# A residual moved from a 128x128 fp32 matmul to two additions on VectorE, in a mixture-of-experts stage

## The chip, the cores and the metric

One core of one Trainium2 chip runs the whole kernel. The metric is device time in microseconds (us). Three runs of the kernel before took 1256.58, 1257.35 and 1257.95 us; their median is 1257.35.

## The reference, cut to what matters

A Mamba block (8 sequences of 1024 rows of 128 numbers) and then a transformer block are applied, each on a normed input, with an outer residual. The Mamba block is not touched by the change except in one preparing step. The transformer block is:

```python
y = layer_norm(x + mha(x), g1, be1)
z = layer_norm(y + moe(y), g2, be2)
# moe: idx = argmax(y @ Wg.T);  for the chosen e:  relu(y @ W1[e] + b1[e]) @ W2[e] + b2[e]
# outer: x = x + norm(z)            (norm without scale and shift)
```

So each row goes to one of 8 experts: 128 -> 512 -> 128, with two biases. What is summed per row is y + relu(y W1 + b1) W2 + b2. Here y = n * g1 + be1, where n is the row normed without scale and shift.

## The kernel before, in words

The five engines each run their own list of instructions: TensorE (PE), VectorE (DVE), ScalarE (ACT), GpSimd (POOL) and SyncE (SP), which issues most DMAs. They meet by semaphores: `wait_ge` holds an engine's whole list until a count is reached. The kernel has three parts: Mamba (to about 880 us), attention (groups of 4x128 rows, 16 groups) and experts.

Attention writes each row, normed but without scale and shift (n), with the row before it (x1) and its number, to a place in HBM (`routed`) that is ordered by expert (GpSimd's scatter, L1868). The experts then read tiles of 128 rows. There are 72 tiles, in 18 quads of 4. The order of the work is written out as slots: in slot s each engine issues its attention work of slot s and then its experts' work of slot s - 65 (`OVERLAP`), so the first experts' tiles run beside the last attention groups. Within an engine the order of the calls in `slot` is the order of issue. Slots of the experts are counted here from their own zero.

Scale and shift of the first norm are folded into the weights before: `fold_w1` into W1 and b1 (with a row of ones made by adding 1.0 to y's transposed copy, so that shifts divided by 128 and summed over 128 rows come out right), and the residual with scale, shift and b2 into one 128x128 fp32 matrix per expert, `w["residual"]` (`residual_base`, L1690 ff., and `residual_weights`, L1401 and L1703 ff.).

A tile t in the experts:

- `load_w1` (SP): copies W1 of the tile's expert to a ring of 4; `load_rows` loads a quad's rows (y, x1, number).
- `turn_y` (PE, L2027): transposes the tile to PSUM; it waits for the copy of the tile before. `copy_yT` (ACT, L2083) copies it to SBUF.
- `hidden` (PE, L2039): 4 fp32 matmuls; `relu` (ACT, L2090).
- `outward` (PE): first the residual matmul yT x `w["residual"]` of the expert (L2059), then 4 fp32 matmuls with W2 (L2063) on top of it, into a quarter of a PSUM bank (3 banks in turn).

Per quad q, from PSUM: `stats_a` (DVE, slot 6 + 4q; L2143 to L2154: four statistics, four aggregations, variance, mean), the inverse root (`root` on GpSimd, slot 8, L2224, for quads 0 to 14; for the last three ScalarE's root and Newton steps on VectorE, `invert`, L2182 ff.), `norm_a` (ACT, L2103, in halves in slots 9 and 10, PSUM -> `zn`), `affine` (DVE, slot 11, L2168 `zg` and L2172 `z`), `stats_b` (DVE, slot 12), root b (GpSimd, slot 13), `norm_b` (ACT, slots 15 and 16, L2114, `z_out`), `add_x1` (DVE, slot 17: `tokens` L2199 and `res` L2200, z_out + x1) and `scatter` (GpSimd, slot 17: 4 indirect DMAs, L2232, one per 128 rows; the indices are `tokens`).

In steady state VectorE's order per four slots is therefore: `stats_a`, `affine` (of the quad before), `stats_b` (of one more before), `add_x1` (of one more). GpSimd's is: root a, root b, four scatters.

Of the kernel before, what the change touches and what calls it, by code (L numbers as in the profile page):

```python
# [19 lines left out]
ALU = mybir.AluOpType  # L20
# [36 lines left out]
def mamba(nc, sem, carrier, banks, sel, ident, half_neg, x, w_in_t, conv_rows, per_channel, w_x_t, w_dt_t, w_out_t, x1, c_rows, late_loads, s_late,  # L57
# [8 lines left out]
    with ctx:  # L66
# [727 lines left out]
        def _(dve):  # L794
# [120 lines left out]
            def split_biases():  # L915

                bres = ygT[0:EXPERTS, :, :].rearrange("p t d -> p (t d)")[:, 0:DF + D]
                bmid = x1t[0:EXPERTS, :, :].rearrange("p t d -> p (t d)")[:, 0:(DF + D) // 2].bitcast(BF16)
                dve.memset(bias_parts[:, :], 0.0)
                dve.tensor_scalar(biases[:, :], biases[:, :], 1.0 / D, None, ALU.mult).then_inc(bias_chain, 1)  # L920
                dve.wait_ge(bias_chain, 1)
                dve.tensor_copy(bias_parts[0:EXPERTS, :], biases[:, :]).then_inc(bias_chain, 1)
                dve.wait_ge(bias_chain, 2)
                dve.tensor_tensor(bres, biases[:, :], bias_parts[0:EXPERTS, :], ALU.subtract).then_inc(bias_chain, 1)
                dve.wait_ge(bias_chain, 3)
                dve.tensor_copy(bmid, bres).then_inc(bias_chain, 1)
                dve.tensor_copy(bias_parts[32:32 + EXPERTS, :], bres).then_inc(bias_chain, 1)
                dve.wait_ge(bias_chain, 5)
                dve.tensor_tensor(bias_parts[64:64 + EXPERTS, :], bres, bmid, ALU.subtract).then_inc(bias_chain, 1)

# [170 lines left out]
def attention(nc, sem, carrier, banks, sel, ident, half_neg, w, shared, x1, v_rows, routed, expert_loads, sb, arena, front, S):  # L1101
# [39 lines left out]
    gap_cols = sb("shift_less_scale_cols", [P, P])  # L1141
    base = sb("residual_base", [P, D])
    gap_row = sb("shift_less_scale_row", [P, D])
    pk = sb("pk", [P, DEEP, GT, ROW])
# [124 lines left out]
    def tensor(pe):  # L1269
# [69 lines left out]
        def turn_y(j):  # L1339
            pe.wait_ge(S["r1_normed"], j + 1)  # L1340
            if j >= 1:
                pe.wait_ge(S["yT_copied"], j)
            else:
                pe.wait_ge(S["w1_folded"], EXPERTS + 2)
            if j == EARLY_GROUPS + 1:
                pe.wait_ge(S["early_chain"], 2)
            if j == EARLY_GROUPS + 2:
                pe.wait_ge(S["early_chain"], EARLY_STEPS)
            for i in range(GT):
                mm = pe.transpose(a3[:, i * P:(i + 1) * P], pk[:, j % DEEP, i, 0:D], ident[:, :])  # L1350
            mm.then_inc(S["y_transposed"], 1)

        def logits(j):
            pe.wait_ge(S["yT_copied"], j + 1)
            if j >= 1:
                pe.wait_ge(S["row_ids"], 5 * (j - 1) + 1)
            else:
                pe.wait_ge(S["gap_chain"], 7)
# [19 lines left out]
        def fold_gate():  # L1378
            pe.wait_ge(S["gap_chain"], 3)
            pe.wait_ge(S["w1_folded"], EXPERTS + 2)  # L1380
            pe.matmul(a2[:, 0:EXPERTS], gap_cols[:, :], w["wg"][:, :], start=True, stop=True)\
              .then_inc(S["weights_summed"], 1)

        def fold_w1(e):
# [5 lines left out]
            if e >= 2:  # L1390
# [4 lines left out]
              .then_inc(S["weights_summed"], 1)  # L1395

        def residual_weights(half):
            pe.wait_ge(S["w1_folded"], EXPERTS - 1 + half)
            for i in range(4):
                mm = pe.matmul((a2, a3)[half][:, i * D:(i + 1) * D], sel[:, 4 * half + i, :],  # L1400
                               w["bias_parts"][:, DF:], start=True, stop=True)  # L1401
            mm.then_inc(S["weights_summed"], 1)

# [31 lines left out]
        def slot(s):  # L1435
            if 0 <= s - 1 < EXPERTS:
                fold_w1(s - 1)
            if s in (9, 10):
                residual_weights(s - 9)
            if s == 16:  # L1440
# [125 lines left out]
    def vector(dve):  # L1566
# [117 lines left out]
        def fold_gate():  # L1684
            scale = w["norm1"][:, 0:1]
            dve.wait_ge(S["weights_summed"], EXPERTS + 3)
# [3 lines left out]
        def residual_base():  # L1690
            scale, shift = w["rows"][:, 2, :], w["rows"][:, 3, :]
            dve.tensor_tensor(gap_row[:, :], shift, scale, ALU.subtract).then_inc(S["gap_chain"], 1)
            dve.tensor_tensor(base[:, :], ident[:, :], scale, ALU.mult).then_inc(S["gap_chain"], 1)
            dve.wait_ge(S["gap_chain"], 5)
            dve.scalar_tensor_tensor(out=base[:, :], in0=gap_row[:, :], scalar=1.0 / D, in1=base[:, :], op0=ALU.mult,
                                     op1=ALU.add).then_inc(S["gap_chain"], 1)
# [6 lines left out]
        def residual_weights(half):  # L1703
            dve.wait_ge(S["gap_chain"], 6)
            dve.wait_ge(S["weights_summed"], EXPERTS + half + 1)
            dve.tensor_tensor(w["residual"][:, 4 * half:4 * half + 4, :],
                              (a2, a3)[half][:, :].rearrange("p (w d) -> p w d", w=4),
                              base[:, :].unsqueeze(1).broadcast_to([P, 4, D]), ALU.add).then_inc(S["w1_folded"], 1)

# [82 lines left out]
        def slot(s):  # L1792
# [94 lines left out]
def experts(nc, sem, banks, sel, ident, half_neg, w, shared, carrier, routed, out, sb, arena, R):  # L1887
# [65 lines left out]
    def sync(sp):  # L1953
# [27 lines left out]
        def load_w1(t):  # L1981
            q, i = divmod(t, 4)
            if t == 0:
                sp.wait_ge(R["w1_folded"], EXPERTS + 2)
                sp.sem_inc(carrier, 1)
# [28 lines left out]
    def tensor(pe):  # L2014
# [29 lines left out]
        def outward(t):  # L2044
            q, i = divmod(t, 4)
            if t == 0:
                pe.wait_ge(R["early_chain"], EARLY_STEPS)
                pe.wait_ge(R["experts_loaded"], 16)
                pe.wait_ge(R["w1_folded"], EXPERTS + 2)
# [28 lines left out]
    def scalar(act):  # L2078
# [18 lines left out]
        def norm_a(q, half):  # L2097
# [42 lines left out]
    def vector(dve):  # L2140
        def stats(src, stat, mv, var_eps, less_mean, s_bn, s_var, s_root, q):
# [3 lines left out]
            dve.wait_ge(s_bn, 2 * q + 1)  # L2145
            dve.sem_inc(carrier, 1)
# [103 lines left out]
def build(nc, x, w_in_t, conv_rows, per_channel, w_x_t, w_dt_t, w_out_t, wqkv_t, bqk, wo_t, wg_t, rows, biases, norm1, w1, w2,  # L2250
# [5 lines left out]
    with ExitStack() as ctx:  # L2256
# [17 lines left out]
        for name, n in TABLE:  # L2274
# [127 lines left out]
```

## Time and profile before

| | |
|---|---|
| three runs | 1256.58, 1257.35, 1257.95 us |
| span of the profiled execution | 1257.2 us (the page gives no other time of it) |
| busy: PE, DVE, ACT, POOL | 89%, 83%, 82%, 80% |
| experts | from about 1058 us (first `hidden`) to the end |
| L2059, residual matmul | x144 entries (two for each fp32 matmul), 27.8 us busy |
| L2232, scatters of the result | x72, 79.9 us busy, mean 1109 ns; 3% of the chain that ended last, its largest share |
| last 4 matmuls of the experts | start at 1225.19 us |
| last scatter | starts 1249.08 us |

The profile is one execution. Times in its rows are counted from the span's start. "Idle before" names what ended an engine's wait. An fp32 matmul has two entries. Entries of the same kind that follow one another are merged in a timeline, as "x4". The chain of waits is followed back from the last instruction, each time to what released it.

### The profile page before, as it was taken

To read this page: it belongs to the slowest core of one execution; us is meant where nothing else is said; L and a number is where in the kernel's file an instruction comes from. 1 tells how busy PE (TensorE), PEld (TensorE's weight loads), DVE (VectorE), ACT (ScalarE), POOL (GpSimd) and SP (SyncE) were. 2 spreads that over 40 slices of the span, in tenths; PEclk is the share of its full clock that TensorE was granted. 3 is DMA by queue.
4 is the path that set the end of the run, shared out by engine and by line. 5 is a ranking of instruction groups with operands and counts; after the bars stand their busy time and mean duration, and the time that the engine had idled before them with its cause. 6 is when DMAs were issued, how large, how long until landed. Compare 5 with 4: busy or idle time off the path is not lost. (4 is left out here: it accounts for less than half of the span.)

```text
span 1257.2 us, 29298 instructions
## 1 busy us (share of the span) xinstructions
PE 1122.1 (89%) x8868; PEld 939.1 (75%) x8868; DVE 1044.1 (83%) x2086; ACT 1025.8 (82%) x2140; POOL 1007.9 (80%) x825
## 2 busy tenths in 40 slices
PE   6799999999999999999999999877799997999990
PEld 2487877877878778787787877877466667989990
DVE  5599999999999999999999999996678887555564
ACT  4899899998998989989899899984479985556672
POOL 6498998989989889898898998986436776678875
PEclk9899999999999999999999999998799999999995
DMA  2223333333333232333333233341465556876640
GB/s 76 85 85 102 101 89 100 99 98 105 88 100 99 96 100 86 113 88 98 103 86 111 79 100 92 101 143 59 126 161 137 159 149 186 258 242 211 204 153 28
DMA packets 149637, 147.65 MB, mean 117 GB/s; under 512 B 46768, under 2 KB 99698, under 8 KB 149518
## 3 DMA queue, kind: packets, MB, share of 16 engines
q1 hardware_dynamic: 144142, 133.64, 36.5%
q0 software_dynamic: 5376, 12.63, 2.9%
q8 instruction: 50, 0.82, 0.3%
q14 instruction: 69, 0.57, 0.2%
HBM read 103.57 MB, written 23.24 MB: 101 GB/s over the span
## 5 line engine op out<-in xcount | busy, mean ns | idle before, releaser
L999 POOL TENSOR_TENSOR cm<-rows_or_blocks 128x1024 f32<-128x1024 f32 x256 | 618.1, 2423 | 81.4 <-DVE rows_or_blocks L834 76.2
L834 DVE TENSOR_TENSOR_SCAN rows_or_blocks<-abuf,hstate,bank 128x512 f32<-128x512 f32 x512 | 613.0, 1259 | 20.8 <-ACT abuf L668 7.4
L462 PE MATMUL bank<-ident,cm 128*128 128x128 f32 x2048 | 256.0, 273 | 2.8 <-POOL cm L999 2.7
L462 PEld LDWEIGHTS bank<-ident,cm 128*128 128x128 f32 x2048 | 230.3, 142 | 3.5 <-POOL cm L999 3.5
L668 ACT ACTIVATE abuf<-delta,aneg 128x512 f32<-128x512 f32 x256 | 166.8, 714 | 2.1 <-DVE rows_or_blocks L834 2.0
L668 ACT ACTIVATE abuf<-xg_or_delta,aneg 128x512 f32<-128x512 f32 x256 | 166.7, 714 | 0.0
L442 PE MATMUL bank<-ident,ub 128*128 128x128 f32 x1024 | 140.6, 279 | 27.1 <-ACT ub L679 16.7
L442 PEld LDWEIGHTS bank<-ident,ub 128*128 128x128 f32 x1024 | 115.7, 142 | 55.4 <-issue 25.7
L359 PE MATMUL bank<-xnT,rows_or_blocks 128*128 128x512 f32 x256 | 125.5, 607 | 1.0 <-ACT halo L596 1.0
L679 ACT ACTIVATE ub<-vs_or_uT,bT 128x256 f32<-128x256 f32 x256 | 108.7, 499 | 0.2
L679 ACT ACTIVATE ub<-uT,bT 128x256 f32<-128x256 f32 x256 | 108.6, 499 | 0.1
L2232 POOL DMA_INDIRECT out<-res,tokens x72 | 79.9, 1109 | 29.6 <-issue 26.6
L1848 POOL TENSOR_TENSOR b_rstd<-b_vare,half_neg 128x4 f32<-128x4 f32 x30 | 30.8, 1027 | 63.9 <-ACT xn_or_u L1483 47.3
L1868 POOL DMA_INDIRECT routed<-pk,desti x64 | 63.1, 986 | 20.3 <-issue 20.3
L2039 PE MATMUL bank<-d_yT,w_of_tile 128*128 128x128 f32 x576 | 76.4, 276 | 0.4 <-issue 0.3
L2063 PE MATMUL bank<-w,hT 128*128 x576 | 76.1, 275 | 0.0
L439 PEld LDWEIGHTS bank<-bdiag,vs_or_uT 128*128 128x128 f32 x512 | 62.1, 191 | 17.6 <-issue 9.1
L439 PEld LDWEIGHTS bank<-bdiag,uT 128*128 128x128 f32 x512 | 62.0, 192 | 16.4 <-issue 8.2
L439 PE MATMUL bank<-bdiag,vs_or_uT 128*128 128x128 f32 x512 | 65.4, 278 | 6.4 <-DVE rows_or_blocks L834 6.3
L2039 PEld LDWEIGHTS bank<-d_yT,w_of_tile 128*128 128x128 f32 x576 | 70.3, 192 | 0.8 <-issue 0.8
L2063 PEld LDWEIGHTS bank<-w,hT 128*128 128x128 f32 x576 | 70.1, 192 | 0.0
L439 PE MATMUL bank<-bdiag,uT 128*128 128x128 f32 x512 | 64.8, 278 | 5.9 <-DVE rows_or_blocks L834 5.9
(298 smaller groups left out, 2114.6 us busy)
## 6 DMA issues: line engine op xcount, KB each, us to landing
rows_or_blocks<-c_rows SPq DMA_DIRECT2D x256, 256.0 KB, 3.2
w_of_tile<-w SPq DMA_DIRECT2D x72, 256.0 KB
rows_or_blocks<-routed SPq DMA_DIRECT2D x72, 128.5 KB
xin<-in_x SPq DMA_DIRECT2D x16, 256.0 KB, 3.6
xres<-in_x SPq DMA_DIRECT2D x16, 256.0 KB, 3.8
x_rows<-x1t SPq DMA_DIRECT2D x16, 256.0 KB, 3.5
xg_or_delta<-x_rows SPq DMA_DIRECT2D x16, 256.0 KB, 3.7
v_rows<-vs_or_uT SPq DMA_DIRECT2D x16, 256.0 KB, 3.4
```

The costliest lines, as they stand in the source:

```text
L359: mm = pe.matmul(bank_xc(f, c)[:, :], w_tap[:, k, c * P:(c + 1) * P], xnT[:, parity(f), k:k + HALF], start=k == 0, stop=k == TAPS - 1)
L439: mm = pe.matmul(dst, uT[parity(g)][:, j, c * P:(c + 1) * P], bdiag[:, n // 4 % 2, j, :], start=True, stop=True)
L442: mm = pe.transpose(dst, ub[:, n // 2 % 2, j, c * P:(c + 1) * P], ident[:, :])
L462: mm = pe.matmul(ps_y[j // 2][:, (j % 2 * CH + c) * P:(j % 2 * CH + c + 1) * P], cm[:, n % CM_RING, c, j * P:(j + 1) * P], ident[:, :], is ...
L668: e = act.activation(abuf[:, n % RING, c, :], delta[parity(g)][:, c, :], ACT.Exp, scale=aneg[:, c, n:n + 1])
L679: i = act.activation(ub[:, n // 2 % 2, j, :], uT[parity(g)][:, j, :], ACT.Copy, scale=bT[:, parity(g), j, n:n + 1])
L834: dve.tensor_tensor_scan(hbuf[:, n % RING, c, :], abuf[:, n % RING, c, :], ps_bx[n % 2 * CH + c][:, :], hstate[:, bass.ds(g * (NST * CH) + ...
L999: pool.tensor_tensor(cm[:, n % CM_RING, :, :], hbuf[:, n % RING, :, :], c, ALU.mult).then_inc(s_cm, 1)
L1868: pool.indirect_dma_start(out=routed[:, :], out_offset=bass.IndirectOffsetOnAxis(ap=desti[:, j % DEEP, i:i + 1], axis=0), in_=pk[:, j % DE ...
L2039: mm = pe.matmul(ps_h[t % 2][:, k * P:(k + 1) * P], w1[:, t % W1_RING, k * P:(k + 1) * P], yT[:, t % YT_RING, :], start=True, stop=True)
L2063: mm = pe.matmul(dst, hT[:, t % 2, k, :], w["w2"][:, bass.ds(e[t], 1), k, :].rearrange("p o d -> p (o d)"), start=False, stop=k == DF // P ...
L2232: pool.indirect_dma_start(out=out[:, :], out_offset=bass.IndirectOffsetOnAxis(ap=tokens[:, q % 2, i:i + 1], axis=0), in_=res[:, q % 2, i, ...
```

## The change

The residual is no longer multiplied. VectorE scales the quad's rows by g1 (`scale_rows`, slot 5 + 4q, after `stats_a` and ahead of `add_x1` in its order) and adds the result to the quad's sums from PSUM (`add_rows`, slot 6 + 4q, ahead of `stats_a`). The row of shifts, be1 + b2[e], is now split into three bf16 parts, stacked at partitions 0, 32 and 64, and added by one bf16 matmul per tile whose stationary operand, `sel`, picks the expert's rows (96 x 128 by 96 x 128). `stats_a` and `norm_a` read the sum from SBUF. The making of the fp32 residual weights in the attention part goes; `split_second_biases` comes (slot 11 of the attention): an addition, a copy, a subtraction, two copies and a subtraction, 8x128 each. `residual_base` was three 128x128 operations on VectorE, `residual_weights` twice 4 bf16 matmuls and a 128x512 addition.

```diff
+        def split_second_biases():
+            chain, parts, second = S["gap_chain"], w["bias_parts"][:, DF:], w["biases"][:, DF:]
+            dve.tensor_tensor(second, second, w["rows"][0:EXPERTS, 3, :], ALU.add).then_inc(chain, 1)
...
-            if s == 6:
-                residual_base()
+            if s == 11:
+                split_second_biases()
-            if s in (10, 11):
-                residual_weights(s - 10)
@@ outward
-                    pe.wait_ge(S["zn_ready"], q - 2)
+                    pe.wait_ge(S["stats_a"], 4 * (q - 2))
             dst = ps_f[q % 3][:, i * D:(i + 1) * D]
-            pe.matmul(dst, yT[:, t % YT_RING, :], w["residual"][:, bass.ds(e[t], 1), :].rearrange("p o d -> p (o d)"),
+            pe.matmul(dst, sel[:, bass.ds(e[t], 1), :].rearrange("p o t -> p (o t)"), w["bias_parts"][:, DF:],
                       start=True, stop=False)
@@ norm_a
-                a = act.activation(zn[:, q % 2, i, :], ps_f[q % 3][:, i * D:(i + 1) * D], ACT.Identity,
+                a = act.activation(zn[:, q % 2, i, :], summed[:, q % 2, i, :], ACT.Identity,
@@ vector
+        def scale_rows(q):
+            n = 4
+            if q == 0:
+                for i in range(4):
+                    dve.wait_ge(S[f"w1_loaded{i}"], 32)
+            else:
+                dve.wait_ge(s_rows[q % 4], 64 * (q // 4 + (q % 4 > 0)))
+                dve.wait_ge(S["stats_a"], 4 * q)
+            dve.tensor_tensor(scaled[:, 0:n, :], rows[:, q % RINGS, 0:n, 0:D],
+                              w["rows"][:, 2, :].unsqueeze(1).broadcast_to([P, n, D]), ALU.mult)\
+               .then_inc(S["stats_a"], 1)
+
+        def add_rows(q):
+            n = 4
+            dve.wait_ge(S["expert_summed"], 4 * q + n)
+            dve.wait_ge(S["stats_a"], 4 * q + 1)
+            if q >= 2:
+                dve.wait_ge(S["zn_ready"], q - 1)
+            dve.tensor_tensor(summed[:, q % 2, 0:n, :], ps_f[q % 3][:, 0:n * D].rearrange("p (i d) -> p i d", i=n),
+                              scaled[:, 0:n, :], ALU.add).then_inc(S["stats_a"], 1)
+
         def stats_a(q):
-            dve.wait_ge(S["expert_summed"], 4 * (q + 1))
+            dve.wait_ge(S["stats_a"], 4 * q + 2)
@@ slot of the experts on VectorE
             for q in due(s, 6):
+                add_rows(q)
                 stats_a(q)
+            for q in due(s, 5):
+                scale_rows(q)
             for q in due(s, 17):
                 add_x1(q)
```

At the start of the kernel the split of the biases (`split_biases`, L914 ff.) now covers the first biases alone, 8x512 instead of 8x640; waits for `w1_folded` ask for 8 instead of 10.

## Rows read from the trace of the kernel before

**Rows 1.** Table by stretch: stretch, length, busy of each engine, clock, DMA share, GB/s

```profile
1066.00:1113.00 47.00, 46.21 (x420) 45.35 (x420) 27.81 (x164) 26.83 (x67) 31.23 (x35) 1.00 0.78 248
...
1157.00:1210.00 53.00, 52.44 (x460) 51.31 (x459) 30.90 (x144) 35.64 (x96) 42.77 (x49) 1.00 0.62 207
```

**Rows 2.** Timeline of GpSimd: start, duration, engine, line, operation, [idle before]

```profile
1113.03 1.05 POOL L2224 TENSOR_TENSOR d_rstd_a<-d_vare_a,half_neg 128x4 f32<-128x4 f32 x1
...
1161.53 1.31 POOL L2232 DMA_INDIRECT out<-res,tokens  x1 [0.30 <-issue]
...
1164.42 1.37 POOL L2232 DMA_INDIRECT out<-res,tokens  x1 [0.30 <-issue]
...
1209.79 1.05 POOL L2224 TENSOR_TENSOR d_rstd_a<-d_vare_a,half_neg 128x4 f32<-128x4 f32 x1
```

**Rows 3.** Timeline of VectorE, the period at 1157

```profile
1160.57 0.69 DVE L2168 TENSOR_TENSOR zg<-zn,row_params 128x512 f32<-128x512 f32 x1 [1.57 <-ACT zn L2103]
1161.29 0.69 DVE L2172 TENSOR_TENSOR z<-zg,row_params 128x512 f32<-128x512 f32 x1
...
1163.61 0.16 DVE L2154 TENSOR_SCALAR d_nmean_b<-d_mv_b 128x4 f32<-128x4 f32 x1
1164.18 0.17 DVE L2199 COPY tokens<-rows_or_blocks 128x4 int32<-128x4 int32 x1 [0.41 <-ACT z_out L2114]
1164.26 0.69 DVE L2200 TENSOR_TENSOR res<-z_out,rows_or_blocks 128x512 f32<-128x512 f32 x1
```

**Rows 4.** Timeline of ScalarE, same period

```profile
1158.37 0.81 ACT L2103 ACTIVATE zn<-bank,d_shift_a,d_rstd_a 128x128 f32<-128x128 f32 x2 [1.67 <-POOL d_shift_a L2226]
1159.07 0.28 ACT L2083 ACTIVATE d_yT<-bank 128x128 f32<-128x128 f32 x1
...
1161.16 0.87 ACT L2114 ACTIVATE z_out<-z,d_shift_b,d_rstd_b 128x128 f32<-128x128 f32 x2
1161.93 0.26 ACT L2083 ACTIVATE d_yT<-bank 128x128 f32<-128x128 f32 x1
```

**Rows 5.** Timeline of TensorE: the table's matmul at 1101, and one tile

```profile
1101.64 0.17 PE L1423 MATMUL bank<-cum_h,ones 128*128 128x8 bf16 x1
...
1101.82 1.06 PE L2039 MATMUL bank<-d_yT,w_of_tile 128*128 128x128 f32 x8
...
1161.58 0.27 PE L2027 MATMUL bank<-ident,rows_or_blocks 128*128 128x128 f32 x1
...
1162.59 0.39 PE L2059 MATMUL bank<-residual_weights,d_yT 128*128 x2
1162.81 1.06 PE L2063 MATMUL bank<-w,hT 128*128 x8
1163.70 0.27 PE L2027 MATMUL bank<-ident,rows_or_blocks 128*128 128x128 f32 x1
```

**Rows 6.** Timeline of GpSimd, where its last wait of the early stage ends

```profile
1100.11 1.52 POOL L2224 TENSOR_TENSOR d_rstd_b<-d_vare_b,half_neg 128x4 f32<-128x4 f32 x1 [2.70 <-ACT z_out L2114]
```

**Rows 7.** Timeline of all engines at 922, attention

```profile
922.57 0.42 PEld L1275 LDWEIGHTS bank<-ident,xn_or_u 128*128 128x128 f32 x4 [0.20 <-ACT xn_or_u L1483]
```

**Rows 8.** Timeline of all engines at 979, attention

```profile
979.45 0.69 DVE L1613 TENSOR_TENSOR o<-bank,rs 128x512 f32<-128x512 f32 x1
979.51 0.96 POOL L1868 DMA_INDIRECT routed<-pk,desti  x1 [0.30 <-issue]
```

**Rows 9.** Timeline of all engines at 1235, the last quads

```profile
1234.97 0.73 DVE L2168 TENSOR_TENSOR zg<-zn,row_params 128x512 f32<-128x512 f32 x1
1234.98 0.97 POOL L2232 DMA_INDIRECT out<-res,tokens  x1 [2.03 <-DVE res L2200]
```

**Rows 10.** Timeline of VectorE, the last quads

```profile
1223.53 0.18 DVE L2182 RECIPROCAL d_guess_a<-d_spread_a 128x4 f32<-128x4 f32 x1 [0.80 <-ACT d_spread_a L2095]
...
1233.42 0.69 DVE L2200 TENSOR_TENSOR res<-z_out,rows_or_blocks 128x512 f32<-128x512 f32 x1
1234.02 0.17 DVE L2182 RECIPROCAL d_guess_b<-d_spread_b 128x4 f32<-128x4 f32 x1
```

More of the change, by code:

```diff
@@ L915, in split_biases @@
             def split_biases():
-                bres = ygT[0:EXPERTS, :, :].rearrange("p t d -> p (t d)")[:, 0:DF + D]
-                bmid = x1t[0:EXPERTS, :, :].rearrange("p t d -> p (t d)")[:, 0:(DF + D) // 2].bitcast(BF16)
+                bres = ygT[0:EXPERTS, :, :].rearrange("p t d -> p (t d)")[:, 0:DF]
+                bmid = x1t[0:EXPERTS, :, :].rearrange("p t d -> p (t d)")[:, 0:DF // 2].bitcast(BF16)
+                first, parts = biases[:, 0:DF], bias_parts[:, 0:DF]
                 dve.memset(bias_parts[:, :], 0.0)
-                dve.tensor_scalar(biases[:, :], biases[:, :], 1.0 / D, None, ALU.mult).then_inc(bias_chain, 1)
+                dve.tensor_scalar(first, first, 1.0 / D, None, ALU.mult).then_inc(bias_chain, 1)
                 dve.wait_ge(bias_chain, 1)
-                dve.tensor_copy(bias_parts[0:EXPERTS, :], biases[:, :]).then_inc(bias_chain, 1)
+                dve.tensor_copy(parts[0:EXPERTS, :], first).then_inc(bias_chain, 1)
                 dve.wait_ge(bias_chain, 2)
-                dve.tensor_tensor(bres, biases[:, :], bias_parts[0:EXPERTS, :], ALU.subtract).then_inc(bias_chain, 1)
+                dve.tensor_tensor(bres, first, parts[0:EXPERTS, :], ALU.subtract).then_inc(bias_chain, 1)
                 dve.wait_ge(bias_chain, 3)
                 dve.tensor_copy(bmid, bres).then_inc(bias_chain, 1)
-                dve.tensor_copy(bias_parts[32:32 + EXPERTS, :], bres).then_inc(bias_chain, 1)
+                dve.tensor_copy(parts[32:32 + EXPERTS, :], bres).then_inc(bias_chain, 1)
                 dve.wait_ge(bias_chain, 5)
-                dve.tensor_tensor(bias_parts[64:64 + EXPERTS, :], bres, bmid, ALU.subtract).then_inc(bias_chain, 1)
+                dve.tensor_tensor(parts[64:64 + EXPERTS, :], bres, bmid, ALU.subtract).then_inc(bias_chain, 1)
             dve.memset(w_x[:, :, RANK:BROW], 0.0)
@@ L1141, in attention @@
     gap_cols = sb("shift_less_scale_cols", [P, P])
-    base = sb("residual_base", [P, D])
-    gap_row = sb("shift_less_scale_row", [P, D])
+    bres = sb("bias_rest", [EXPERTS, D])
+    bmid = sb("bias_middle", [EXPERTS, D], BF16)
     pk = sb("pk", [P, DEEP, GT, ROW])
@@ L1343, in turn_y @@
             else:
-                pe.wait_ge(S["w1_folded"], EXPERTS + 2)
+                pe.wait_ge(S["w1_folded"], EXPERTS)
             if j == EARLY_GROUPS + 1:
@@ L1357, in logits @@
             else:
-                pe.wait_ge(S["gap_chain"], 7)
+                pe.wait_ge(S["gap_chain"], 10)
             for i in range(GT):
@@ L1395, in fold_w1 @@
               .then_inc(S["weights_summed"], 1)
[L1397 to L1402, printed above, removed]
         def early_table(part):
@@ L1437, in slot @@
                 fold_w1(s - 1)
-            if s in (9, 10):
-                residual_weights(s - 9)
             if s == 16:
@@ L1685, in fold_gate @@
             scale = w["norm1"][:, 0:1]
-            dve.wait_ge(S["weights_summed"], EXPERTS + 3)
+            dve.wait_ge(S["weights_summed"], EXPERTS + 1)
             dve.scalar_tensor_tensor(out=gate[:, :], in0=w["wg"][:, :], scalar=scale, in1=a2[:, 0:EXPERTS],
                                      op0=ALU.mult, op1=ALU.add).then_inc(S["gap_chain"], 1)
[L1690 to L1696, printed above, removed]
+        def split_second_biases():
+            chain, parts, second = S["gap_chain"], w["bias_parts"][:, DF:], w["biases"][:, DF:]
+            dve.tensor_tensor(second, second, w["rows"][0:EXPERTS, 3, :], ALU.add).then_inc(chain, 1)
+            dve.wait_ge(chain, 4)
+            dve.tensor_copy(parts[0:EXPERTS, :], second).then_inc(chain, 1)
+            dve.wait_ge(chain, 5)
+            dve.tensor_tensor(bres[:, :], second, parts[0:EXPERTS, :], ALU.subtract).then_inc(chain, 1)
+            dve.wait_ge(chain, 6)
+            dve.tensor_copy(bmid[:, :], bres[:, :]).then_inc(chain, 1)
+            dve.tensor_copy(parts[32:32 + EXPERTS, :], bres[:, :]).then_inc(chain, 1)
+            dve.wait_ge(chain, 8)
+            dve.tensor_tensor(parts[64:64 + EXPERTS, :], bres[:, :], bmid[:, :], ALU.subtract).then_inc(chain, 1)
         def fold_w1(e):
@@ L1701, in fold_w1 @@
                                      in1=(a2, a3)[e % 2][:, :], op0=ALU.mult, op1=ALU.add).then_inc(S["w1_folded"], 1)
[L1703 to L1708, printed above, removed]
         def clear_small():
@@ L1901, in experts @@
     hT = sb("hT", [P, 2, DF // P, P])
+    scaled = sb("rows_scaled", [P, 4, D])
+    summed = sb("rows_and_expert", [P, 2, 4, D])
     zn = sb("zn", [P, 2, 4, D])
@@ L1983, in load_w1 @@
             if t == 0:
-                sp.wait_ge(R["w1_folded"], EXPERTS + 2)
+                sp.wait_ge(R["w1_folded"], EXPERTS)
                 sp.sem_inc(carrier, 1)
@@ L2048, in outward @@
                 pe.wait_ge(R["experts_loaded"], 16)
-                pe.wait_ge(R["w1_folded"], EXPERTS + 2)
+                pe.wait_ge(R["gap_chain"], 9)
             if t == EARLY_TILES:
@@ L2140, in vector, with stats @@
     def vector(dve):
-        def stats(src, stat, mv, var_eps, less_mean, s_bn, s_var, s_root, q):
+        def stats(src, stat, mv, var_eps, less_mean, s_bn, at, s_var, s_root, q):
             for i in range(4):
@@ L2144, in stats @@
             b.then_inc(s_bn, 1)
-            dve.wait_ge(s_bn, 2 * q + 1)
+            dve.wait_ge(s_bn, at + 1)
             dve.sem_inc(carrier, 1)
@@ L2151, in stats @@
                 dve.wait_ge(s_root, root_steps(q))
-            dve.wait_ge(s_bn, 2 * q + 2)
+            dve.wait_ge(s_bn, at + 2)
             dve.tensor_scalar(var_eps[:, :], mv[:, :, 1], EPS, None, ALU.add)
             dve.tensor_scalar(less_mean[:, :], mv[:, :, 0], -1.0, None, ALU.mult).then_inc(s_var, 1)
+        def scale_rows(q):
[17 more added lines that the diff above has]
+                              scaled[:, 0:n, :], ALU.add).then_inc(S["stats_a"], 1)
         def stats_a(q):
-            dve.wait_ge(S["expert_summed"], 4 * (q + 1))
-            stats(lambda i: ps_f[q % 3][:, i * D:(i + 1) * D], stat_a, mv_a, vare[0], nmean[0], S["stats_a"],
+            dve.wait_ge(S["stats_a"], 4 * q + 2)
+            stats(lambda i: summed[:, q % 2, i, :], stat_a, mv_a, vare[0], nmean[0], S["stats_a"], 4 * q + 2,
                   S["variance_a"], S["roots_a"], q)
@@ L2175, in stats_b @@
             dve.wait_ge(S["z_ready"], q + 1)
-            stats(lambda i: z[:, q % 2, i, :], stat_b, mv_b, vare[1], nmean[1], S["stats_b"], S["variance_b"],
+            stats(lambda i: z[:, q % 2, i, :], stat_b, mv_b, vare[1], nmean[1], S["stats_b"], 2 * q, S["variance_b"],
                   S["roots_b"], q)
```

3 lines of the change are left out of this document (1 added, 2 removed).

## The prediction

> **What bounds the kernel now.** I read the page first, then the table by stretch, the chain of waits, and then the timelines of single engines. The change touches the experts alone (1058 us to the end) and a few instructions of the attention. In the table TensorE looks like the bound of both long stretches of the experts: busy 46.21 of 47 us at first, 52.44 of 53 us later [rows 1]. That is true of the first only. From 1113 us on the chain of waits runs over GpSimd: its eleven rounds from root to root last (1209.79 - 1113.03) / 11 = 8.80 us per quad of four tiles [rows 2], while TensorE needs 4 x 2.12 = 8.48 us for them [rows 5]. TensorE is slowed to that pace through ScalarE, which stands still 1.67 us a round before `zn` for GpSimd's root [rows 4], with the next `copy_yT` queued behind it.
>
> GpSimd is not simply full. Two of its four scatters last 1.31 and 1.37 us [rows 2]; undisturbed ones last 0.97 us [rows 9]. The first of the two starts 0.24 us after `z` started on VectorE and the second 0.16 us after `res` [rows 3]: both start while VectorE adds two operands from SBUF, and both end 0.85 us after that addition does. So the round is a loop through both engines. From the start of the root: 1.37 to `zn` (1158.37 against 1157.00, one round before 1165.80, where the fourth scatter ends), 2.20 to `zg`, 0.72 to `z`, 2.32 to the last of `stats_b`, 0.57 to `tokens` (0.41 of it a wait for `z_out`), 0.08 to `res`, 0.69 for it, 0.85 to the scatter's end: 8.80 us [rows 2 to 4].
>
> **The change, part by part.** Terms are against the profiled span of 1257.2 us; the runs' median, 1257.35, lies 0.15 above it, and I add the sum to the median.
>
> *TensorE.* The residual's fp32 matmul takes 1162.81 - 1162.59 = 0.22 us of a tile of 2.12; four fp32 ones take 0.89, so the turn takes 0.12 [rows 5]. No bf16 matmul of 128 columns between fp32 ones is shown. The nearest is the table's of 8 columns: with it the turn and it take 0.18, so it costs 0.06, and the other 120 columns at 2.4 GHz (granted clock 1.00) are at most 0.05 more. I take 0.09, a gain of 0.13 a tile (bounds 0.10 and 0.16). It counts only where TensorE sets the pace, up to GpSimd's last real wait, 2.70 us for `z_out` of the first quad [rows 6]; from there GpSimd is loaded without a gap. That `z_out` stands in slot 16 of the experts, after 15 tiles' sums; the first two tiles' gain runs into the wait for the loaded rows of the second quad. 13 x 0.13 = 1.7 us; the DMA engines are 0.78 busy here [rows 1] and the faster tiles will meet some waits, so I take 1.3 us (0.5 to 2.1). From there to the end TensorE's gain is worth nothing: it ends in a longer wait.
>
> *ScalarE.* `norm_a` reads SBUF instead of PSUM. From `zn`'s first half to the next instruction it is 0.70 us, from `z_out`'s, which reads SBUF, 0.77 [rows 4]. With half of that again in the second half `zg` comes 0.11 later.
>
> *VectorE, per round.* `scale_rows` has two operands from SBUF like `z`, so 0.69 us, and the next instruction starts 0.60 after it [rows 10]. In VectorE's order it stands behind `stats_b` and ahead of `add_x1`: `tokens` and `res` are queued behind it, and the scatter waits for them. It waits for nothing itself. `add_rows` costs 0.72 (0.69 and the step to `stats_a`, as from `zg` to `z` [rows 3]). Before `stats_a` VectorE waits for TensorE, and the variance that it gives is used a round later, so `add_rows` is hidden; its cover is the 1.57 us of wait before `zg` [rows 3], and without it, it would cost 0.72 a round. `scale_rows` is not hidden: it takes the 0.41 us wait before `tokens` and more. The loop becomes 1.37 + 2.31 + 0.72 + 2.32 + 0.08 + 0.60 + 0.08 + 0.69 + 0.85 = 9.02 us, 0.22 more than now, 11 times: +2.4 us (bounds in the rivals: -0.3 and +0.6 a round).
>
> A two-operand addition holds up GpSimd. The one from PSUM doesn't: `o` started 0.06 before a scatter, ran 0.63 into it, and that lasted 0.96 [rows 8]. The Trainium skill ("SBUF — State Buffer", Who interferes with whom) draws the same line: VectorE with two SBUF inputs contends with a GpSimd instruction that reads SBUF, with one input it does not. It also infers that such an addition leaves the writing of DMA descriptors alone; by that half the scatters would not be delayed, a round would stay at 8.80 and the sum would be +0.6. The 1.37 beside 0.97 us speaks against it: an indirect DMA has indices to read.
>
> *The end.* From quad 15 on the roots leave GpSimd and VectorE is full, but for 0.80 us [rows 10], until `res` of quad 15; the last twelve scatters start 0.87 us after that (1234.98 against 1234.11) and run in a row [rows 9, 10]. Two `scale_rows` and two `add_rows` fall into this stretch, 2 x 0.60 + 2 x 0.72 = 2.6 us, `zn` adds 0.1, and the 0.80 takes part of it: +1.9 us (1.2 to 2.7). TensorE's earlier end is no help, since the sums wait for VectorE then.
>
> *Attention.* Gone are eight small bf16 matmuls, two additions of 0.69 us like `o` [rows 8], three 128x128 operations; six 8x128 ones come, at 0.16 to 0.2 each [rows 3]. They lie where the next turn on TensorE waits for ScalarE's `xn` anyway [rows 7], and `less_max` behind them has room. I take 0, between -0.8 (all removed work on the path) and +1.2 (all of the new). The start-up's narrower splits lie ahead of a wait of VectorE: 0.
>
> Sum: -1.3 + 2.4 + 1.9 = +3.0, so 1260.3 us.
>
> **Rivals.** *GpSimd reads first (not slower).* The place is the fourth scatter of the round. It starts 3.13 after `z` started (1164.42 - 1161.29) and will again, since it hangs on the second scatter, which ends with `z`; `res` starts now at 2.97 and then at 2.32 + 0.08 + 0.60 + 0.08 = 3.08: only 0.05 ahead instead of 0.16. At 0.16 VectorE wins [rows 2, 3]; at 0.01 GpSimd won, with 0.97 us [rows 9]. The point from which it decides lies between. If GpSimd wins, the round is 8.80 - 0.34 - 0.40 + 0.45 = 8.5 us (both lengthenings gone, the first back and 0.11 longer): 11 x -0.3 = -3.3, and -1.3 - 3.3 + 1.9 = -2.7: 1254.7. For it: the margin is as small as my error. Against: the margin is still on VectorE's side. The skill's page (same section) says that whichever starts first keeps the port for its whole instruction, which would have VectorE win here, 1260.3.
> *The addition from PSUM contends too.* It would lie over the next root: up to 0.4 a round, 11 x 0.4 = 4.4 more: 1264.7. Rows 8 speak against it.
> *The bf16 matmul gives nothing*, because the fp32 weights behind it load no faster: no 1.3 at the start, 1261.6. The 0.06 of the table's matmul speaks against it.
> *The new addition falls where no scatter starts*, and `res` keeps its place: a round stays at 8.80, +0.6, 1258.0. Against it is the order on VectorE.
>
> **How the numbers follow.** Forecast 0.48 (its own range 1258.3 to 1262.3), GpSimd first 0.27, PSUM contends 0.07, no gain of the matmul 0.08, round unchanged 0.10. The range of 8 in 10 reaches to the faster case and leaves out most of the PSUM case: 1253.8 to 1262.6. About 0.2%, 2.5 us, can be told from no change. Slower by more: 0.3 of the forecast's 0.48, and the two cases above it, 0.44. Faster by more: 0.2 of the second case's 0.27 and a little of the last, 0.22. The rest, 0.34, is the same.
>
> **What would show it.** TensorE's tile at 1.99 us in the early stretch; GpSimd's last early wait ending 1.3 us sooner; rounds of 9.0 us with a fourth scatter of some 1.5 us, with `tokens` right behind `scale_rows` and no wait; `zg` 2.31 behind `zn`; `zn` rows near 0.48; no wait of VectorE from quad 15's root to `res` 15, and that 1.9 us later against the last root on GpSimd. A fourth scatter of 0.97 would be the first rival; a root of 1.4 the second. Wrong altogether I would be if the rounds left GpSimd, with TensorE or VectorE full instead.

## The result, and the profile after

The changed kernel takes 1260.98 us (median of 12 runs, 1258.75 to 1262.97) against 1256.96 of the kernel before (12 runs, 1254.83 to 1258.81): ratio 1.003, interval 1.0021 to 1.0038, so 4.0 us slower, between 2.6 and 4.8. Forecast was 1260.3, 3.0 us slower. The profiled execution after took 1261.45 us with a span of 1259.6. In every later run whose span is on record the time is 1.7 to 1.9 us above the span, so the profiled execution of the kernel before, with its span of 1257.2, took about 1259.0 us (an estimate): 2.0 more than the median of its runs.

The table by stretch, after (columns as in [rows 1]):

```profile
1066.00:1113.00 47.00, 43.61 (x401) 42.94 (x401) 33.33 (x166) 26.73 (x67) 31.79 (x36) 1.00 0.78 249
1157.00:1210.00 53.00, 48.77 (x428) 47.35 (x427) 37.48 (x156) 36.05 (x96) 42.83 (x48) 1.00 0.61 204
```

TensorE has lost 2.6 and 3.7 us of work in the two stretches, VectorE has gained 5.5 and 6.6; GpSimd has the same 42.8 us in the second. Why TensorE's relief doesn't show in the time can be read from one round, that is from one root a to the next (root a is the inverse root of `stats_a` on GpSimd, once per quad). Timelines of one round, after: first GpSimd's (start, duration, engine, line, operation),

```profile
1156.61 1.05 POOL L2238 TENSOR_TENSOR d_rstd_a<-d_vare_a,half_neg 128x4 f32<-128x4 f32 x1
...
1161.13 1.43 POOL L2246 DMA_INDIRECT out<-res,tokens  x1 [0.30 <-issue]
1162.86 0.98 POOL L2246 DMA_INDIRECT out<-res,tokens  x1 [0.30 <-issue]
1164.14 1.48 POOL L2246 DMA_INDIRECT out<-res,tokens  x1 [0.30 <-issue]
1165.62 1.07 POOL L2238 TENSOR_TENSOR d_rstd_a<-d_vare_a,half_neg 128x4 f32<-128x4 f32 x1
```

then VectorE's,

```profile
1156.33 0.69 DVE L2164 TENSOR_TENSOR rows_and_expert<-bank,rows_scaled 128x512 f32<-128x512 f32 x1 [0.58 <-PE bank L2053]
...
1160.29 0.69 DVE L2179 TENSOR_TENSOR zg<-zn,row_params 128x512 f32<-128x512 f32 x1 [1.48 <-ACT zn L2093]
1161.02 0.69 DVE L2183 TENSOR_TENSOR z<-zg,row_params 128x512 f32<-128x512 f32 x1
...
1163.41 0.69 DVE L2154 TENSOR_TENSOR rows_scaled<-rows_or_blocks,row_params 128x512 f32<-128x512 f32 x1
1164.01 0.16 DVE L2210 COPY tokens<-rows_or_blocks 128x4 int32<-128x4 int32 x1
1164.08 0.68 DVE L2211 TENSOR_TENSOR res<-z_out,rows_or_blocks 128x512 f32<-128x512 f32 x1
```

then ScalarE's and TensorE's.

```profile
1157.97 0.88 ACT L2093 ACTIVATE zn<-rows_and_expert,d_shift_a,d_rstd_a 128x128 f32<-128x128 f32 x2 [2.05 <-POOL d_shift_a L2240]
1158.76 0.26 ACT L2073 ACTIVATE d_yT<-bank 128x128 f32<-128x128 f32 x1
```

```profile
1162.14 0.22 PE L2049 MATMUL bank<-bias_parts,sel 96*128 96x128 bf16 x1
1162.20 1.11 PE L2053 MATMUL bank<-w,hT 128*128 x8
1163.14 0.27 PE L2017 MATMUL bank<-ident,rows_or_blocks 128*128 128x128 f32 x1
...
1165.15 0.27 PE L2017 MATMUL bank<-ident,rows_or_blocks 128*128 128x128 f32 x1
```

A round is 1165.62 - 1156.61 = 9.01 us. `scale_rows` (L2154) has pushed `tokens` and `res` back, the wait before `tokens` in [rows 3] is gone, `res` starts 0.06 ahead of the fourth scatter, and this scatter lasts 1.48 us; the second scatter, 0.11 behind the start of `z`, lasts 1.43. Both end 0.86 and 0.85 us after the addition. `add_rows` (L2164) stands behind a wait of 0.58: hidden. ScalarE's wait for the root has grown from 1.67 to 2.05 us: TensorE's relief ends in a longer wait.

Not every round is like this one. Of the eleven, four at the start take 8.50, 9.15, 8.52 and 9.57 us, six take 9.01 to 9.03, and one takes 8.66: there `res` comes 0.26 behind the fourth scatter, and this lasts 1.12. I call the ones of 9.01 to 9.03 settled.

The landmarks of both kernels, each profiled twice (the second pair, `g1` and `g2`, ran on one chip; it is told below), in us; "root a 3" is the start of root a of quad 3, and the eleven rounds go from there to root a 14:

| | first tile's turn | root a 3 | root a 14 | last scatter | span |
|---|---|---|---|---|---|
| before, rows 1 to 10 | 1056.9 | 1113.03 | 1209.79 | 1249.08 | 1257.2 |
| after | 1056.2 | 1111.84 | 1210.36 | 1251.49 | 1259.6 |
| before again (`g1`) | 1055.6 | 1111.54 | 1205.05 | 1245.83 | 1254.0 |
| after again (`g2`) | 1054.8 | 1110.03 | 1208.24 | 1249.37 | 1257.5 |

First pair: -1.2 up to root a 3, +1.8 in the rounds, +1.8 in the end, sum +2.4. Second pair: -1.5, +4.7, +0.3, sum +3.5. The sums are the differences of the spans. The last scatters of after (GpSimd) and what they wait for (VectorE):

```profile
1237.41 0.97 POOL L2246 DMA_INDIRECT out<-res,tokens  x1 [2.75 <-DVE res L2211]
...
1251.49 0.97 POOL L2246 DMA_INDIRECT out<-res,tokens  x1 [0.30 <-issue]
```

```profile
1235.78 0.16 DVE L2210 COPY tokens<-rows_or_blocks 128x4 int32<-128x4 int32 x1
1235.85 0.69 DVE L2211 TENSOR_TENSOR res<-z_out,rows_or_blocks 128x512 f32<-128x512 f32 x1
```

`res` of quad 15 is 25.49 us behind root a 14; it was 23.63 in [rows 2, 10].

### The profile page after: what moved, and what is told of

It reads as the page before. It is cut to its first block and busy times, and to the rows that moved or that the text cites. A ratio compares the mean times of both kernels' runs of the same rounds, so it can differ in the third digit from the quotient of the medians.

```text
span 1259.6 us, 29210 instructions
## 1 busy us (share of the span) xinstructions
PE 1116.4 (89%) x8788; PEld 933.0 (74%) x8788; DVE 1065.3 (85%) x2123; ACT 1027.4 (82%) x2140; POOL 1011.3 (80%) x825
## 5 line engine op out<-in xcount | busy, mean ns | idle before, releaser
L1836 POOL TENSOR_TENSOR b_rstd<-b_vare,half_neg 128x4 f32<-128x4 f32 x30 | 30.7, 1023 | 65.3 <-ACT xn_or_u L1475 43.7
L2053 PE MATMUL bank<-w,hT 128*128 x576 | 80.7, 284 | 0.0
```

The lines of the kernel that those rows point to most:

```text
L2053: mm = pe.matmul(dst, hT[:, t % 2, k, :], w["w2"][:, bass.ds(e[t], 1), k, :].rearrange("p o d -> p (o d)"), start=False, stop=k == DF // P ...
```

## The experiments

**The theory:** an instruction of GpSimd that starts just after a VectorE addition of two SBUF operands is held up until some 0.85 us after that addition's end; the change costs 0.22 us a round because `scale_rows` lengthens the loop that goes through this. **The rival:** the round is longer because VectorE's chain is, wherever `res` falls.

Edits are shown against the changed kernel where nothing else is said.

**On two slower chips.** The first eight kernels ran on chips on which the kernel before takes 1299.86 us (the four of `e`; median of 35 runs) and 1306.5 us (the four of `f`; 35 runs). Single runs of one kernel differ by up to 18 us there, so an interval is 5 to 8 us wide and can't show the 1 to 3 us that most of the expectations speak of.

*The matmul alone* (`e1`, repeated as `f1`). The residual is left out of the computation, neither multiplied nor added:

```diff
-                    pe.wait_ge(S["stats_a"], 4 * (q - 2))
+                    pe.wait_ge(S["zn_ready"], q - 2)
...
-                a = act.activation(zn[:, q % 2, i, :], summed[:, q % 2, i, :], ACT.Identity,
+                a = act.activation(zn[:, q % 2, i, :], ps_f[q % 3][:, i * D:(i + 1) * D], ACT.Identity,
...
-                add_rows(q)
                 stats_a(q)
-            for q in due(s, 5):
-                scale_rows(q)
```

`stats_a` reads the sums from PSUM again, too.

> The changed kernel without scale_rows and add_rows: the bf16 one-hot matmul stays, stats_a and norm_a read PSUM again, so the output lacks the residual. Theory of three terms (start -1.3, rounds +0.22 x 11, end +1.9, the last two by VectorE's additions): only the start's gain is left. The round at GpSimd is 8.80 us again, the tile of TensorE about 2.0 us, the total 1 to 2 us under the kernel before (some 1255.6), with the last scatter 1 to 2 us earlier than before. Rival (TensorE sets the pace of the experts after all, as its busy share says): 72 tiles x 0.11 us = 8 us under the kernel before. Rival (the fall of TensorE's clock to 0.50 near 1115 us, after a longer idle time, costs time): it is here too, and the kernel is no faster than before.

> The kernel of e1_matmul_only once more, on another chip: there the kernel before took 1300 us, TensorE stood still for 0.7 us a quad at its table of experts, and rounds of 10 us hid what was to be seen. The expectation is the same: about 1.3 us under the kernel before if only the start's gain is left, rounds of 8.80 us, tile of 2.0 us; 8 us under it if TensorE set the pace.

Measured: 1298.7 us, 0.9986 (0.9954 to 1.0018), and 1305.2, 0.9996 (0.9968 to 1.0023): neither can be told from no change. 8 us less, as the rival of `e1` has it, is excluded.

*`scale_rows` a quad early* (`e2`, `f2`), right behind `stats_a` of the quad before, so that it no longer stands between `stats_b` and `tokens`:

```diff
+                if q == 0:
+                    scale_rows(0)
                 add_rows(q)
                 stats_a(q)
-            for q in due(s, 5):
-                scale_rows(q)
+                if q + 1 < QUADS:
+                    scale_rows(q + 1)
```

> The changed kernel with one move: scale_rows of the next quad is issued right behind stats_a, where VectorE waits for zn (1.48 us), instead of between stats_b and add_x1. Same work, same result. Theory (its place in the loop is what it costs): tokens waits for z_out again, the round goes from 9.02 back to about 8.85 us, 11 rounds give 1.5 to 2 us, and the end some 0.6: 2 to 2.5 us under the changed kernel. Rival (VectorE's load as such costs): same time as the changed kernel within 0.5 us.

> The kernel of e2_scale_early once more. Theory (place in the loop): rounds of about 8.85 instead of 9.02 us, 2 to 2.5 us under the changed kernel, so 0.1% over the kernel before. Rival (load as such): 0.3% over it, as the changed kernel.

Measured: 1299.48, 1.0005 (0.9979 to 1.003), and 1304.41, 0.9981 (0.9959 to 1.0003): neither can be told from no change.

*`res` later than the scatter's start* (`e3`, `f3`), by two idle statistics on VectorE behind `tokens`:

```diff
+            if q < BY_POWER:
+                for k in range(2):
+                    dve.bn_stats(spare[:, k, :], w["rows"][:, 4, :])
```

> The changed kernel with more work on VectorE: two statistics of a constant 128x128 tile (0.2 us each) between tokens and res, quads 0 to 14. Theory (GpSimd's fourth scatter is held up because res starts just before it): res now starts 0.35 us after that scatter, which takes 0.97 instead of 1.48 us; the round falls from 9.02 to about 8.5 us and the total by 4 to 5.5 us, to about 1256. Rival (no such hold-up; VectorE's chain is simply longer): 0.4 us more a round, 11 x 0.4 = 4.4 us slower than the changed kernel.

> The kernel of e3_res_late once more. Theory (hold-up of the fourth scatter): rounds of about 8.5 us, the fourth scatter 0.97 us, 1 us under the kernel before. On the slow chip both lengthenings were gone and it was the only one clearly under the kernel before (0.9961). Rival (longer chain): rounds of 9.4 us, 8 us over the kernel before.

Measured: 1295.29, 0.9961 (0.9936 to 0.9986), and 1299.94, 0.996 (0.9932 to 0.9987). With more work on VectorE this is the only version whose interval lies below the kernel before there, both times: the rival, which asked for 8 us over it in `f3`, is wrong there too. Why it is below isn't shown, since its rounds (9.9 to 10.0 us) are not the expected 8.5.

*The additions alone* (`e4`). The one-hot matmul is replaced by an fp32 one of the old size, so the sum is another one:

```diff
-            pe.matmul(dst, sel[:, bass.ds(e[t], 1), :].rearrange("p o t -> p (o t)"), w["bias_parts"][:, DF:],
+            pe.matmul(dst, yT[:, t % YT_RING, :], w["w2"][:, bass.ds(e[t], 1), 0, :].rearrange("p o d -> p (o d)"),
```

> The changed kernel with a 128x128 fp32 matmul in the place of the bf16 one (yT by the first quarter of W2 of the expert, so its sum is wrong): VectorE's additions alone, TensorE as before. Theory of three terms: the start's gain goes, rounds and end stay: about 1.3 us over the changed kernel, some 5.3 over the one before; tile of TensorE 2.12 us, round 9.0 us. Rival (TensorE's gain is worth more than the start): 3 us or more over the changed kernel.

Measured: 1302.38, 1.0014 (0.9983 to 1.0044): no change that can be told.

*The kernel before with `res` late* (`f5`), the same two statistics.

> The kernel before, its residual by the fp32 matmul, with only the same two idle statistics (0.2 us each) between tokens and res, quads 0 to 14. Theory: the fourth scatter takes 0.97 instead of 1.37 us, the round falls from 8.80 to TensorE's 8.48 us: 11 x 0.3 = 3.3 us under the kernel before, although VectorE only does more. Rival (no hold-up): 0 to 4.4 us over it.

Measured: 1307.23, 1.0014 (0.9993 to 1.0035): not the 3.3 us less that the theory gave.

On these chips the rounds are another matter: 9.9 to 10.6 us on the mean (root a 3 to root a 14) instead of the 8.5 to 9.02 of the expectations, bound by something that the first chip doesn't show. `e1`, TensorE from 1110 to 1250 us by groups (busy, mean ns, idle before and its releasers), and one of its rows:

```profile
L2053 PE MATMUL bank<-w,hT 128*128 x424 | 60.1, 285 | 4.4 <-issue 4.4
L2017 PE MATMUL bank<-ident,rows_or_blocks 128*128 128x128 f32 x53 | 15.6, 294 | 19.7 <-ACT d_yT L2073 19.7
```

```profile
1130.67 1.15 PE L2053 MATMUL bank<-w,hT 128*128 x8 [1.59 <-issue]
```

and `f5`, the same groups of the kernel before:

```profile
L2064 PE MATMUL bank<-w,hT 128*128 x408 | 57.0, 284 | 20.0 <-ACT hT L2091 12.6 <-issue 7.3
```

TensorE stands still ahead of `outward` with no releaser to be seen, 0.7 to 1.6 us at a time, in both kernels; after, on the first chip, has 0.0 there in the same stretch. What it waits for stays open, and it is the smaller part: these waits are 4.4 us in `e1`, those for `d_yT` 19.7 (9.0 in after, on the first chip). What these runs do tell: `e1` and `f1` need 41.95 and 41.96 us from root a 14 to the last scatter, `e2`, `f2` and `e4` with the additions 43.8 to 44.3, so the two passes on VectorE cost some 2 us in the end stage. (`f5`, with the fp32 matmul and idle statistics, needs 47.59; the kernel before itself has no profile there.) They don't price the rounds, neither for the theory nor against it, so I went back to a chip like the first.

**On a chip like the first** (kernel before: 1256.39 us, 29 runs), all four together. *Both kernels unchanged* (`g1` one execution, `g2`).

> The kernel before, for a second profile beside the next three. Theory, if this chip runs it in about 1257 us: rounds of 8.80 us, second and fourth scatter 1.3 and 1.37 us. If it runs it in 1300 us as the chips of the runs so far, TensorE stands still at the first residual matmul of a quad and the rounds are 10 us or more, set by TensorE; then the lengthened scatters are rare, and this profile is the base for the others.

> The changed kernel once more. On a chip like the first: +3 us, rounds of 9.02, start 1.2 earlier, end 1.9 later. On a slow chip, where TensorE sets the rounds: the rounds cost nothing (or gain the matmul's 0.1 us a tile, up to 5 us in all), the end still costs 1.9 us: ratio 0.997 to 1.002. Rival (the additions cost wherever they stand, by VectorE's load): 1.003 there too.

Measured: `g1` 1255.74; `g2` 1259.91, 1.0025 (1.0015 to 1.0036). The changed kernel has the rounds of its first profile: 8.93 on the mean, 9.00 to 9.03 when settled, and again a single one of 8.65. The kernel *before* does not: its eleven rounds take 8.50 instead of 8.80. The chain that ended last, its share by engine, from the page of the first profile of before and from that of `g1`:

```profile
PE 7%; issue 7%; POOL 6%; ACT 5%; DVE 2%; SPq 1%; DMA 1%; POOLq 0%; ACTq 0%; DVEq 0%
```

```profile
PE 15%; ACT 5%; issue 3%; DVE 3%; POOL 1%; DMA 1%; POOLq 0%; SPq 0%; DVEq 0%; ACTq 0%
```

One round of `g1`, GpSimd, VectorE and ScalarE:

```profile
1154.18 1.06 POOL L2224 TENSOR_TENSOR d_rstd_a<-d_vare_a,half_neg 128x4 f32<-128x4 f32 x1
...
1158.71 1.40 POOL L2232 DMA_INDIRECT out<-res,tokens  x1 [0.30 <-issue]
...
1161.69 0.97 POOL L2232 DMA_INDIRECT out<-res,tokens  x1 [0.30 <-issue]
1162.67 1.06 POOL L2224 TENSOR_TENSOR d_rstd_a<-d_vare_a,half_neg 128x4 f32<-128x4 f32 x1
```

```profile
1158.56 0.69 DVE L2168 TENSOR_TENSOR zg<-zn,row_params 128x512 f32<-128x512 f32 x1 [0.55 <-ACT zn L2103]
...
1162.87 0.19 DVE L2199 COPY tokens<-rows_or_blocks 128x4 int32<-128x4 int32 x1 [1.09 <-ACT z_out L2114]
1162.95 0.68 DVE L2200 TENSOR_TENSOR res<-z_out,rows_or_blocks 128x512 f32<-128x512 f32 x1
```

```profile
1157.73 0.80 ACT L2103 ACTIVATE zn<-bank,d_shift_a,d_rstd_a 128x128 f32<-128x128 f32 x2
...
1161.97 0.87 ACT L2114 ACTIVATE z_out<-z,d_shift_b,d_rstd_b 128x128 f32<-128x128 f32 x2
```

`res` starts 8.77 us after root a, where it was 1164.26 - 1157.01 = 7.25 in the round of [rows 3]. It comes only when the fourth scatter is done, and this lasts 0.97. GpSimd then needs 8.49 us (8.06 and one lengthening of 0.43), TensorE 4 x 2.12 = 8.48, and `zn` has no wait for the root: TensorE paces ScalarE, ScalarE's `z_out` keeps `res` back. So the kernel before has two patterns with the same code. The expectation of `g1`, rounds of 8.80 with a long fourth scatter, was wrong.

*`res` late in the changed kernel* (`g3`, the edit of `e3`).

> The kernel of e3_res_late a third time, for the first time beside the changed kernel. Theory (hold-up): fourth scatter 0.97 us; on a chip like the first rounds of 8.5 us and 4 to 5 us under the changed kernel, on a slow one 0 to 3 us under it. Rival (longer chain): over the changed kernel by 4 us on a chip like the first, by 0 to 4 on a slow one.

Measured: 1259.24, 1.0018 (1.0007 to 1.0028): 0.7 us under the changed kernel, where 4 to 5 were expected. The round is as expected. One of them, GpSimd and VectorE:

```profile
1166.84 1.42 POOL L2250 DMA_INDIRECT out<-res,tokens  x1 [0.30 <-issue]
1168.56 0.97 POOL L2250 DMA_INDIRECT out<-res,tokens  x1 [0.30 <-issue]
1169.83 0.97 POOL L2250 DMA_INDIRECT out<-res,tokens  x1 [0.30 <-issue]
1170.81 1.07 POOL L2242 TENSOR_TENSOR d_rstd_a<-d_vare_a,half_neg 128x4 f32<-128x4 f32 x1
```

```profile
1169.12 0.69 DVE L2155 TENSOR_TENSOR rows_scaled<-rows_or_blocks,row_params 128x512 f32<-128x512 f32 x1
...
1169.79 0.48 DVE L2214 BATCH_NORM_STATS2 spare<-row_params 128x6 f32<-128x128 f32 x2
1170.19 0.73 DVE L2215 TENSOR_TENSOR res<-z_out,rows_or_blocks 128x512 f32<-128x512 f32 x1
```

VectorE does 0.4 us more in a round, `res` starts 0.36 behind the fourth scatter, this lasts 0.97, and the round falls from 9.01 to 8.50 (1162.31 to 1170.81). The rival is refuted for the round: with its longer chain the round would have grown. Over eleven rounds it is 8.60 on the mean, 3.7 us less than `g2`; but the end stage takes 42.27 instead of 41.13 (the last of the idle statistics fall into it) and the start 0.5 more. The profiled span is 2.0 us shorter; the medians of `g3` and `g2` differ by 0.7 only (the means by 1.4), with runs of `g3` from 1256.95 to 1260.98, so the profiled run, 1257.29, is one of its faster ones. The cause is shown in the rows and hardly in the time.

*Both meetings avoided* (`g4`): `e2`'s move, two idle statistics between `zg` and `z`, two before `res`.

> The changed kernel with scale_rows of the next quad behind stats_a, two idle statistics between zg and z, and two between tokens and res, quads 0 to 14: neither z nor res then starts just before a scatter. Theory: all four scatters 0.97 to 1.04 us, rounds of about 8.1 us on a chip like the first (GpSimd's own time, 8.80 - 0.34 - 0.40), 10 us under the changed kernel and 6 under the one before; on a slow one the fastest of the four all the same. Rival: 0.8 us more of VectorE's work a round costs up to 9 us.

Measured: 1258.82, 1.0015 (1.0006 to 1.0024): 1.1 us under the changed kernel instead of 10. Rounds of 8.06 us appear, with all scatters after the first at 0.97: GpSimd's own time. But every second round or so is 9.1 to 9.5. Where it goes wrong, GpSimd and VectorE:

```profile
1166.89 0.97 POOL L2255 DMA_INDIRECT out<-res,tokens  x1 [0.31 <-issue]
1167.87 1.32 POOL L2247 TENSOR_TENSOR d_rstd_a<-d_vare_a,half_neg 128x4 f32<-128x4 f32 x1
...
1171.33 1.21 POOL L2255 DMA_INDIRECT out<-res,tokens  x1 [0.62 <-issue]
```

```profile
1167.62 0.67 DVE L2218 TENSOR_TENSOR res<-z_out,rows_or_blocks 128x512 f32<-128x512 f32 x1
...
1170.93 0.69 DVE L2155 TENSOR_TENSOR rows_scaled<-rows_or_blocks,row_params 128x512 f32<-128x512 f32 x1
```

`res` now meets the root (1.32 instead of 1.05, it started 0.25 after `res`) and the moved `scale_rows`, 0.40 ahead, the first scatter (1.21 instead of 1.04). Fixed padding doesn't hold the two engines apart; with a mean round of 8.65 and a start 3.5 us longer than in `g2` (1056.9 to 1115.63), nothing is won. No version tried beats the kernel before on this chip. `e2`'s move alone and `f5`'s late `res` in the kernel before were not run on this chip, so that `scale_rows` costs by its place in the loop rests on the rows of the round and on no run of its own.

## Why the prediction was right, point by point

- **Start, -1.3.** A tile on TensorE takes 2.01 us, not 1.99: the fp32 matmuls start 0.06 after the bf16 one, but take 0.94 instead of 0.89, so it costs 0.11 where I took 0.09. Up to root a 3 the profiles are 1.2 and 1.5 us earlier, but 0.7 and 0.8 of that is there before the experts' first tile. I put attention at 0, and two profiles of the kernel before differ by 1.3 at the same point, so that part can't be told from no change. Within the experts it is -0.5 and -0.7: over-sized. In the first pair the second quad waits longer for its rows, 2.14 us instead of 0.45; the second pair doesn't show that wait.
- **Rounds, +0.22.** Every term of the loop came out: `zn` 1.36 after the root's start, `zg` 2.32 after that, `tokens` 0.60 and `res` 0.67 behind `scale_rows`, the scatter's end 0.86 after `res`'s: 9.02 predicted, 9.00 to 9.03 in the settled rounds of two profiles. That five of eleven rounds are others makes the term +1.8 instead of +2.4 in the first pair. `g3` shows that the hold-up is the cause of the long fourth scatter. It was the comparison that failed: I took 8.80 as *the* round of before, from one profile in which it is constant. In `g1` it is 8.50, and the term is +4.7.
- **Which starts first.** I put `res` 0.05 ahead of the fourth scatter; it is 0.06, and VectorE wins. The margin was as thin as I feared: in the six profiles of the two faster chips a scatter that starts 0.01 or 0.02 behind such an operation lasts 0.96 or 0.97, all that start 0.04 to 0.49 behind are lengthened, and of three at 0.03 two are (1.50 and 1.51) and one is not (0.98). The first rival (round 8.5) is thus wrong for the changed kernel, but its pattern, a fourth scatter of 0.97, is the one in which the kernel *before* runs in `g1`, only with `res` behind that scatter, not beside it. The Trainium skill ("SBUF — State Buffer", Who interferes with whom) infers that such additions leave the writing of DMA descriptors alone; here the scatter's 1.48 us with `res` 0.06 ahead of it, against 0.97 with `res` 0.36 behind (`g3`), says otherwise for an indirect DMA with its indices in SBUF. The Trainium skill ("SBUF — State Buffer", Summary: rules for kernel authors) also says that with two SBUF inputs against a GpSimd instruction that reads SBUF the second to start is blocked until the first is done. Here that holds one way only: where GpSimd is first, VectorE's instruction isn't held, and takes 0.67 to 0.75 us beside a scatter (`res` 0.73 in the round of `g3`) against 0.67 to 0.69 alone.
- **`add_rows` and the PSUM rival.** It starts 0.28 ahead of root a, which lasts 1.05: no contention. `res`, two operands from SBUF, 0.25 ahead of the root in `g4` makes it 1.32. The second rival is wrong.
- **"The matmul gives nothing"** is wrong too: 0.11 a tile, and [rows 5]'s turn to turn of 2.12 is now 2.01.
- **End, +1.9.** +1.84 in the first pair, and about 2 on the other chips. Against `g1` it is +0.35: there TensorE paces the rounds of before, and its end stage is 1.5 us longer.
- **The sum.** +2.4 and +3.5 by profile, +4.0 and +3.5 by the medians, +3.0 forecast. I added terms read against a span of 1257.2 to a median that belongs to faster executions (about 1259.0 against 1256.96 us, see above). The two patterns of the kernel before seem to lie in its own runs: of the 29, 16 are 1253.88 to 1256.84 and 13 are 1257.72 to 1259.94, with none between, and the profile I read would be of the upper kind. That the two groups of runs are the two patterns is an inference from one profile each.
- **What was luck.** In the first pair the start was over-sized within the experts by 0.8 us and the rounds by 0.6 the other way, and 0.7 us were gained ahead of the experts, where I had put 0. Against the other pattern of before the rounds cost twice what I wrote and the end almost nothing, and the sum moved by 1.1 us only. The mechanism of the settled round was right; that the sum came so near was in part luck.

Why does after not fall into the pattern of 8.50? In `g1` it is held there by TensorE at 8.48 us a round against GpSimd's 8.49. With 4 x 2.01 = 8.04 that hold is gone: `zn` waits 2.05 us for the root again and `res` comes early. Both profiles of after begin with such rounds (8.50, then 9.15; 8.52 and 8.36, then 9.53) and then leave them for 9.0. So the faster TensorE may itself have cost something. That is argued from the rows and not shown; `e1`, which could have shown it, ran on slower chips only.

## What to carry to other kernels

Before moving work from one engine to another, follow the loop that sets the round: here the relief of TensorE, 0.11 us a tile, counted at most where TensorE set the pace, and 0.60 us on VectorE in front of one instruction cost more. Where two engines hold each other up, a shift by hundredths of a microsecond can decide about 0.5 us a round, and padding of a fixed length moves the meeting to another instruction. And profile the kernel before more than once: a round that is constant within one execution can have another constant value in the next.

## What the runs showed of the hardware

- In the six profiles of the two faster chips, from 1040 us on, 123 scatters and 22 roots of GpSimd start 0.04 to 0.49 us after a VectorE addition or multiplication (128x512, fp32) with two SBUF operands. Every scatter ends 0.82 to 0.93 us after the end of that operation and lasts up to 1.49 us instead of 0.97; every root ends 0.87 to 0.91 after it and lasts up to 1.55 instead of 1.05. Scatters that start ahead of it aren't lengthened (`g3`, 0.36 ahead: 0.97), nor those beside an addition with one operand in PSUM (13 scatters of 0.96 and 1.04; 1.04 is what the first of four lasts without one, too).
- TensorE's clock fell after a wait. Timeline row and table by stretch, after:

```profile
1114.28 0.47 PE L2017 MATMUL bank<-ident,rows_or_blocks 128*128 128x128 f32 x1 [3.49 <-ACT d_yT L2073]
```

```profile
1112.00:1116.00 4.00, 1.72 (x8) 1.72 (x9) 0.87 (x4) 2.45 (x7) 3.22 (x5) 0.71 1.04 254
1116.00:1120.00 4.00, 4.00 (x21) 3.94 (x20) 2.98 (x13) 1.64 (x4) 3.08 (x4) 0.50 0.47 158
```

  It stood still 3.49 us and then ran at the lower of its two levels (0.50 is 1.2 GHz). In `g1` it fell to 0.52 (1115 to 1118 us) after a wait of 2.58 us; in the first profile of before, after one of 2.57, it kept 1.00. What this costs isn't shown: the first four rounds of after take 35.74 us and four settled ones 36.08, but they differ in the meetings of scatters too.
- From chip to chip the same program differs by 3 to 4%: 1256.39 against 1299.86 and 1306.5 us. Up to 800 us TensorE's busy time agrees to 0.3 us between `e1` and `g1`; of the 43.7 us between their spans 23.4 have arisen by root a 3 and 19.2 come in the rounds. The reason isn't shown. Which version is best differs too: `e3` is 0.4% below the kernel before there, and 0.2% above it here (`g3`).
